# A graph layer pair on one core: 65 gather slots in place of 60, and the fullest tile's work moved behind the next indices

## What is computed

```python
h = jnp.maximum(_layernorm(x, axis=-1), 0.0)
# layer 1: attention over the neighbours, 4 heads of 32
Wh = (h @ W).reshape(N, H, D)
e = s_src[:, None, :] + s_dst[None, :, :]
e = jnp.where(e >= 0, e, ALPHA * e)
e = jnp.where(adj[:, :, None] > 0, e, NEG_INF)
attention = jax.nn.softmax(e, axis=1)
h_prime = jnp.einsum('ijh,jhd->ihd', attention, Wh)
x = x + jax.nn.elu(h_prime.reshape(N, H * D))
# layer 2: maximum over the neighbours
h = jnp.maximum(_layernorm(x, axis=-1), 0.0)
masked = jnp.where(mask[:, :, None], h[None, :, :], neg)
x = x + jnp.max(masked, axis=1)   # 0 where there is no neighbour
```

## Time and profile before

| | us |
|---|---|
| median of 3 runs | 491.2 (489.4 to 493.13) |
| the profiled execution, its own time | 493.0 |
| its span, first to last instruction | 491.0 |
| GpSimd busy | 328.1 (67%) |
| VectorE busy | 314.0 (64%) |
| TensorE products busy | 303.5 (62%) |
| ScalarE busy | 141.5 (29%) |

### The profile page before, as it was taken

How to read it: one execution, slowest core, us unless ns; L and a number is a source line. 1 busy time by engine, 2 the same in 40 slices (tenths; PEclk the granted TensorE clock), 3 DMA queues, 4 the chain that set the end, 5 groups by cost and what they waited for, 6 DMA issues and landing times. The chain is left out here.

```text
span 491.0 us, 6636 instructions
## 1 busy us (share of the span) xinstructions
PE 303.5 (62%) x2017; PEld 225.1 (46%) x2017; DVE 314.0 (64%) x1219; ACT 141.5 (29%) x330; POOL 328.1 (67%) x360
## 2 busy tenths in 40 slices
PE   0966567679789687689464521464565655466664
PEld 0833334266346353355354520354564544365653
DVE  6998876859869596779846382455444545454553
ACT  1653422131544538173733160010110101010111
POOL 6972673704777777767777225777777777777770
PEclk9989579689789699788775785588857788875688
DMA  7998699996999999993575011222222222222221
GB/s 263 420 368 348 237 319 380 404 366 237 369 342 371 404 400 404 403 401 124 183 245 165 12 66 53 53 55 53 58 56 63 66 65 64 73 62 75 69 72 45
DMA packets 28731, 100.86 MB, mean 205 GB/s; under 512 B 6869, under 2 KB 13397, under 8 KB 20501
## 3 DMA queue, kind: packets, MB, share of 16 engines
q1 hardware_dynamic: 16245, 76.33, 39.7%
q0 software_dynamic: 9344, 19.75, 15.6%
q10 hardware_dynamic: 3104, 4.33, 2.4%
HBM read 93.92 MB, written 6.46 MB: 204 GB/s over the span
## 5 line engine op out<-in xcount | busy, mean ns | idle before, releaser
L741 POOL DMA_INDIRECT G<-wh_table,idx x146 | 149.1, 1022 | 81.2 <-issue 43.3
L1641 POOL DMA_INDIRECT G<-h_table,idx x146 | 138.2, 946 | 49.1 <-issue 44.2
L1735 DVE TENSOR_TENSOR_SCAN S<-adjf,S,psf 128x512 f32<-128x512 bf16 (+2 forms) x38 | 45.9, 1209 | 85.8 <-PE psf L1666 76.0
L927 PE MATMUL psf<-adjf,packw 128*128 128x512 f16 x256 | 77.4, 446 | 17.5 <-DMA adjf<-in_adj_dram 12.9
L1666 PE MATMUL psf<-identf,G 128*128 128x128 f32 x146 | 31.8, 352 | 81.9 <-DMA G<-h_table,idx 81.9
L1651 ACT COPY Sb<-psf 128x512 f32<-128x512 f32 (+2 forms) x39 | 21.8, 558 | 168.4 <-PE psf L1674 168.4
L1666 PEld LDWEIGHTS psf<-identf,G 128*128 128x128 f32 x146 | 20.0, 173 | 90.4 <-DMA G<-h_table,idx 90.4
L1686 PE MATMUL psf<-Sb,OL 128*128 128x128 f32 x292 | 55.3, 351 | 0.3 <-DVE rows_out L1721 0.2
L1082 PE MATMUL psf<-G,OQ 128*128 128x132 f32 x292 | 48.6, 321 | 7.0 <-issue 5.0
L1686 PEld LDWEIGHTS psf<-Sb,OL 128*128 128x128 f32 x292 | 52.5, 268 | 0.7 <-issue 0.4
L927 PEld LDWEIGHTS psf<-adjf,packw 128*128 128x128 f16 x256 | 24.8, 107 | 55.6 <-issue 17.9
(11 more groups left out here) (188 smaller groups left out, 481.0 us busy)
## 6 DMA issues: line engine op xcount, KB each, us to landing
adjf<-in_adj_dram SPq DMA_DIRECT2D x64, 1024.0 KB, 11.5
adjf<-keep_table SPq DMA_DIRECT2D x4, 960.0 KB, 7.3
G<-wh_table,idx POOLq DMA_INDIRECT x146
G<-h_table,idx POOLq DMA_INDIRECT x146, 2.6
out_dram<-rows_out SPq DMA_DIRECT2D x32, 64.0 KB, 1.7
wh_table<-OQ ACTq DMA_DIRECT2D x7, 272.0 KB, 8.4
h_table<-h1b ACTq DMA_DIRECT2D x3, 384.0 KB, 2.3
xsf<-in_x_dram SPq DMA_DIRECT2D x2, 512.0 KB, 10.3
```

The costliest lines, as they stand in the source:

```text
L741: pool.indirect_dma_start(G[:, plan.at[k] + b, :], None, wh_table, bass.IndirectOffsetOnAxis(ap=idx[:, n:n + 1], axis=0)).then_inc(gathere ...
L927: nc.tensor.matmul(o, packw[:, k, :], bits, start=(k == 0), stop=False)
L1641: pool.indirect_dma_start(G1[:, g % NG, q, :], None, h1_table, bass.IndirectOffsetOnAxis(ap=idx[:, n0 + q:n0 + q + 1], axis=0)).then_inc(f ...
L1735: V.tensor_tensor_scan(S[:, g % 3, 0:w * P], flags[:, n0 * P:(n0 + w) * P], ps[:, g % 3, 0:w * P], start, ALU.mult, ALU.max).then_inc(scan ...
```

## The change

It changes no operation's arithmetic. It does four things.

- **Slots.** The ring has 65 blocks. Batch 4 gets slots of its own (50 to 64) and waits for no one (`free_after` -1). Batch 5 takes the hub's and waits for the hub's sum in place of batch 2's; batches 6 to 9 wait for the same batches as before. To make room `cand` moves into `near`, `prod` into `em`, and the rows that are stored move from `h1b` into the buffer of the exponentials, which alternates between `ex` and a part of `E2` (`ex_of`), with one store semaphore for each. `elus(k)` now waits until the store from the same buffer two batches before has landed.
- **Hub scores and maxima.** `scores(0)` and `scores(1)` move from the end of turns 1 and 2 to behind the masks of turns 2 and 3; `maxima` of both move behind `edges`, and the hub's `less_max` behind `take_words(3, 2)`. TensorE does `scores_by_row` of the hub behind `select` and `turn` and the hub's `max_back` right after, in turn 3.
- **Hub weighing and sums.** `weigh(1)` moves to turn 4, behind the indices of batch 4, with `weigh(2)` behind it; `aggregate(1)` follows in turn 4 of TensorE ahead of `aggregate(2)`.
- **Hub's end.** `finish(1)` stands at the end of turn 4, `finish_rest(1)` at the start of turn 5; GpSimd does the norms of the hub and of batch 2 both ahead of batch 5, and `h1_out(1)` comes in turn 5.

The core of the diff, without the renamed semaphores and the lines of ScalarE that follow the same order:

```diff
-        users = [[0, 1]] + [[k] for k in range(2, self.nb)]
...
-        self.ring = sum(room)
+
+        hubs, gap = self.size[0] + self.size[1], self.size[2] + self.size[3]
+        third = hubs + gap + self.size[4] - self.size[7]
+        self.at = [0, self.size[0], hubs, hubs + self.size[2], hubs + gap, 0, max(self.size[5:]), third, 0, max(self.size[5:])]
+        self.free_after = [-1, -1, -1, -1, -1, 1, 3, 4, 5, 6]
+        self.ring = hubs + gap + self.size[4]
...
-        cand = sbl("cand", [P, UK * BITS], I32)
+        assert SIZE * P >= 2 * UK * BITS
+        cand = near[:, :].bitcast(I32)[:, 0:UK * BITS]
...
-        prod = E2[:, 0:SK]
+        prod = em[:, :, :].rearrange("p k h -> p (k h)")[:, 0:SK]
...
-        h1b = sbl("h1b", [P, U, D])
...
+        def ex_of(k):
+
+            n = len(plan.tiles(k))
+            if k == 1:
+                return ex[:, U - n:U, :]
+            return E2[:, U * D:(U + n) * D].rearrange("p (t d) -> p t d", d=D) if k % 2 else ex[:, 0:n, :]
...
             for k in range(NBT + 3):
-                tl = plan.tiles(k - 3)
-                if tl:
-                    pool.wait_ge(var1_ready, 2 * (k - 3))
+                for j in (1, 2) if k == 5 else (k - 3,) if k > 5 else ():
+                    tl = plan.tiles(j)
+                    pool.wait_ge(var1_ready, 2 * j)
...
                     act.wait_ge(hp_ready, k)
-                    nc.scalar.activation(ex[:, 0:len(tl), :], hp[:, 0:len(tl), :], ACT.Exp).then_inc(ex_ready, 1)
+                    if k > 3:
+
+                        act.wait_ge(h1_stored[k % 2], 16 * ((k - 1) // 2))
+                    nc.scalar.activation(ex_of(k), hp[:, 0:len(tl), :], ACT.Exp).then_inc(ex_ready, 1)
...
                 pack_to(words_free(k - 1, 3))
-                if k <= NBT:
+                if 2 <= k - 2 <= NBT - 2:
                     max_back(k - 2)
                 if k < NBT:
                     select(k)
                     turn(k)
+                if 0 <= k - 2 < 2:
+                    scores_by_row(k - 2)
+                if k == 3:
+                    max_back(1)
...
-                    aggregate(k - 2)
+                    if k == 4:
+                        aggregate(1)
+                    if k - 2 > 1:
+                        aggregate(k - 2)
...
-                    if 0 <= k - 1 < NBT:
+                    if 2 <= k - 1 < NBT:
                         scores_by_row(k - 1)
...
-                together(*when(plan.tiles(k - 3), finish, k - 3))
+                if k == 5:
+                    together(finish_rest(1))
+                together(*when(k > 4 and plan.tiles(k - 3), finish, k - 3))
                 if k == 0:
                     split_scores()
-                together(*when(new, rows_of_edges, k), *when(0 <= k - 2 < NBT, distances_to_max, k - 2))
+                together(*when(new, rows_of_edges, k), *when(2 <= k - 2 < NBT, distances_to_max, k - 2))
+                together(*when(0 <= k - 2 < 2, scores, k - 2))
...
-                together(*when(plan.whole(k - 2), weigh, k - 2))
+                together(*when(k - 2 > 2, weigh, k - 2))
                 together(*when(new, edges, k))
+                if k == 4:
+                    together(weigh(1))
+                    together(weigh(2))
                 if 2 <= k < NBT:
                     line_ends(k)
+                together(*when(0 <= k - 2 < 2, maxima, k - 2))
...
                 take_words(k, 2)
+                together(*when(k - 2 == 1, less_max, k - 2))
                 take_words(k, 3)
                 together(*when(k + 1 < NBT, extract, k + 1))
-                together(*when(0 <= k - 1 < NBT, scores, k - 1))
+                if k == 4:
+                    together(finish(1))
+                together(*when(2 <= k - 1 < NBT, scores, k - 1))
```

More of the change, by code:

```diff
@@ L911, in _ @@
             h1_out(NBT - 1)
-            act.wait_ge(h1_stored, 16 * (NBT - 1))
+            for b in range(2):
+                act.wait_ge(h1_stored[b], 16 * len(range(2 - b, NBT, 2)))
         @block.tensor
```

45 lines of the change are left out of this document (24 added, 21 removed).

## The result

Measured side by side, the changed kernel takes 495.48 us (median of 11 runs, 491.78 to 497.17) and the kernel before 493.06 (11 runs, 489.05 to 496.65). The ratio is 1.0064, 95% interval 1.0035 to 1.0094: about 3.1 us slower. The profiled execution took 495.38 us, span 493.5, against a span of 491.0 before. The forecast was 1.1 us faster. A ratio leaves out runs that took over 1.5% longer than the fastest of their kernel, a median doesn't.

The account below looks back on a forecast made before the run. The prediction took second-pass gathers, begun after a first pass paced from about 160 us by the adjacency stream, as the bound. Stream -2.8, first pass's end +1.7, second pass 0 gave -1.1: 490.1 us against 491.2, range 486 to 495.

Parts of the forecast that it names:

- Indices, batches 3 and 4: First pass, GpSimd's gathers: batch 3 starts 11.0 us earlier at 104.6, batch 4 8.1 us earlier at 128.9.
- The hub's sums and pack 16: Turn 4 on TensorE: hub's sums begin at 129.6, take 5.67 us, and pack 16 is done at 141.0, not earlier.
- Turn 5: First pass on VectorE: turn 5 starts at 138.9, plus 1.5 us for the hub's exponentials.
- The stream: Adjacency loads pacing the first pass: earlier packs close holes before 126 us, gaining 2.8 us, between 0 and 5.7.
- End of the first pass: Last exponentials share a buffer and wait for batch 7's store: 1.7 us later, bounds 0 and 2.5.
- Second pass: The gathers of the second pass: untouched by the change, 0 us.
- Edits at nothing: Shared buffers (`cand` in `near`, `prod` in `em`), earlier store waits and batch 4's dropped wait cost nothing.
- The lead: Faster rival, chance 0.17: GpSimd's 8.1 us lead at batch 4 reaches the end, giving 484.8 us.
- Only the end changes: Rival, chance 0.20: pack 16 holds the stream to its present time, its term is 0, giving 492.9 us.
- The slower rival: Chance 0.11: hub's sums on TensorE at half clock take 12.3 us, pack 16 done at 147.7, giving 496.9 us.
- own range: Range of the forecast's sum alone, without the rivals: 487.5 to 493 us.
- The rule on the stream: By the skill's 435 GB/s ceiling, the stream has 3.3 us of headroom and follows an earlier packer: 486.8 us.

Follow-up runs that it names:

- e6: The changed kernel, unchanged, as a control on one chip with the kernel before; ratio 1.0088 to the kernel before.
- e4: The changed kernel with 22 extra products keeping TensorE busy in three idle stretches of turns 3 and 4; ratio 1.005 to the kernel before.
- the second pair: The kernel before (e5) and the changed kernel (e6), both unchanged, measured and traced on one chip; ratios 1.0015 and 1.0088.
- e7: The changed kernel with pack 16 ahead of the hub's sums, batch 5's offsets behind them, and own room for the last exponentials; ratio 1.0049 to the kernel before.
- e3: The changed kernel with the last batch's exponentials in room of their own, not waiting for batch 7's store; ratio 1.0023 to the kernel before.
- e1: Only the change's 65 slots and shared buffers, every stage in the order of the kernel before; ratio 1.0012 to the kernel before.
- e12: Slots and shared buffers in the order of the kernel before, plus own room for the last exponentials; ratio 1.0005 to the kernel before.
- e18: The same version as e12, run again; ratio 1.0008 to the kernel before.
- e11: As e7, and VectorE no longer waits at turn 5's start for the hub's exponentials; ratio 1.0012 to the kernel before.
- e5: The kernel before, unchanged, as a control with a trace of its own; ratio 1.0015 to itself.
- e8: As e7, with pack 17 also moved ahead of tile 1's sums on TensorE; ratio 1.013 to the kernel before.
- e2: The changed kernel with tile 14's words ahead of the hub's weighing and pack 16 ahead of the hub's sums; ratio 1.004 to the kernel before.

## Why the prediction was wrong, step by step

*Indices, batches 3 and 4.* Batch 3 was forecast at 104.6 and came at 105.9, batch 4 at 128.9 and came at 130.1, turn 4 at 118.1 and came at 119.2, the hole for the offsets was forecast as 5 us and was 5.28. Right, all 1.1 to 1.3 us late, though not by one lag. Batch 3 is late because turn 3 starts 1.0 us late. Turn 4 is late because pack 12 ran at half clock (3.27 + 0.60 us in place of 1.98 + 0.38). The hub's row sums went the other way: 5.26 us was their time at half clock, and they took 2.94. That they leave turn 4 only 1.1 us late is luck.

*The hub's sums and pack 16.* Forecast done at 141.0, measured 144.5. The hub was forecast to be weighed at 129.6 and was so at about 131.7 (127.89 plus 3.82): the lag of 1.1, and 1.0 us more because VectorE waited 2.52 us for a transpose behind pack 14, which ran at half clock (3.14 us). The sums began at 132.71, another 1.0 later, since pack 15 at half clock (3.60 + 0.60 in place of 1.98 + 0.38) held TensorE that long. The sums themselves took 6.22 in place of 5.67. I had looked for the clock's effect in the hub's sums alone. And pack 15 should have been read, not assumed: it ran at half clock in the kernel before too. Timeline of TensorE of the kernel before, then of e6, where it ran at full clock and the sums waited 1.34 us for the weighing:

```profile
130.32 3.60 PE L927 MATMUL psf<-adjf,packw 128*128 128x512 f16 x8 [2.12 <-ACT psf L749]
```

```profile
130.39 1.98 PE L945 MATMUL psf<-adjf,packw 128*128 128x512 f16 x8 [2.12 <-ACT psf L754]
```

The loss of e6 is no smaller (1.0088 against 1.0064), and e4 gained little, so this clock doesn't look like what lost the time.

*Turn 5.* This step fails: "Turn 5 starts at 138.9, plus 1.5 us for the hub's exponentials". The 138.9 answers to the scores of batch 3, measured at 140.37: late by little more than the lag. Between them and turn 5's first instruction the kernel before has 1.2 us (142.28 to 143.5) and the changed one 5.1 (140.4 to 145.5). The addition was 3.9, not 1.5: a wait of 2.77 and 1.0 of `finish_rest`, which I had struck from turn 4 and not put back. ScalarE's queue shows why the wait is long. The values were there at 140.0, but the exponentials stand behind the copy of tile 1's sums, the end lines and the sum of tile 15's words (that copy, then the exponentials):

```profile
141.85 0.27 ACT L854 COPY ag<-psf 128x132 f32<-128x132 f32 x1 [2.44 <-PE psf L1105]
...
143.29 0.29 ACT L846 ACTIVATE ex<-hp_f 128x128 f32<-128x128 f32 x1
```

So turn 5 starts 2.0 us later than in the kernel before (145.5 against 143.5, and 146.2 against 144.2 in the second pair), not 3 us earlier.

*The stream.* This term of the sum fails with it. The -2.8 rested on the two holes before 126 us, and those closed as forecast. It failed by what comes after: I took pack 16 for the only thing that could give the gain back, and read off turn 5 only its offsets. In the changed kernel pack 16 did open the hole (DMA share 0.43 in 138 to 147 us). But packs 18 and 19 stand behind turn 5's `select`, and e7 shows that with pack 16 out of the way they open another. The forecast of tile 27 near 200 was 204.34. In place of -2.8 the first pass was 0.8 us longer in one pair and 3.1 in the other. How much of that is turn 5's start stays open.

*End of the first pass.* Forecast +1.7. The wait before the last exponentials is 2.42 in place of 0.71 us, the stretch 1.45 longer, and own room takes the wait away (e3, e7). Right. The stretch of the second pair is 3.88 longer, for a reason that I had not foreseen (TensorE's clock, below).

*Second pass.* Forecast 0, measured -0.4 and 0.0.

*Edits at nothing.* Right within what the ratios tell: e1, e12, e18.

*The rivals.* The lead didn't carry through: 7.0 us at batch 4 (8.1 forecast), gone by batch 5. "Only the end changes" was nearer than the forecast and still lacked turn 5's start. The slower rival named the right place: pack 16 came behind 144, and there are holes in 142 to 150 us. But its price was the hub's sums at 12.3 us, and they took 6.2 (5.6 in e6, up to 8.2 in the slower groups); and the date that it hung on doesn't decide (e4, e11). No rival was the exponentials' wait, although the forecast carries its 1.5 us in a half sentence. I had given that half sentence no bound from above.

*The time itself.* The forecast of 490.1 stood on a median of 491.2 from three runs; eleven runs put it at 493.06. So of the 5.4 us between forecast and 495.48, 1.9 belong to the base and 3.5 to the change. The "own range" of 487.5 to 493 was also narrower than the bounds of its two terms, which give 485.5 to 493.7.

*The rule on the stream.* By it the stream would have had headroom and followed an earlier packer. It ran at 401 GB/s in 160 to 203 us as before, so no run used such headroom there, though other stretches ran faster (412 GB/s in 106 to 109 us and 425 in 116 to 119 of the changed kernel).

## What to carry to other kernels

A wait that is removed from one engine of a ring of stages was worth nothing here, since the ring was no shorter: add up that engine's idle time over all turns that the work was moved across, before and after (23.4 and 23.4 us here), and price each wait that the new order brings at the turn's boundary. Work that is postponed past a boundary carries its tail along: here the exponentials, the residual sum and one more norm. And where freed buffers are reused by a late stage, look at the last user, behind which nothing is left to hide a store.

## What the runs showed of the hardware that I had not expected

*TensorE's clock and short waits.* In the changed kernel pack 15 ran at half rate (3.60 us for 8 products, the lower level, 1.2 GHz) behind an idle time of only 1.76 us, and the granted clock was 0.52 in 120 to 126 us, ahead of it. But a low clock ahead isn't needed. In the kernel before, it was 1.00 in 120 to 126 us and 0.94 in 126 to 130; then TensorE idled 2.12 us, and pack 15 took 3.60 too. In e6 the same pack behind the same 2.12 us took 1.98. With 22 extra products in the idle stretches (e4) it took 1.98 behind 1.25 us. So a pause of some 2 us can cost the clock or not, in the same place of the program, and the rows don't show what decides. The Trainium skill ("TensorE: Matmul & The Clock Gate", "What's actually happening") says that the array falls to 1.2 GHz after idling, and that fits these rows; my reading of it, that a short pause does no harm, does not.

The clock also sets the end of the first pass. In its first trace TensorE idled 4.16 us ahead of the last scores and the next six products took 1.53 us; in e5 it had no such idle time and six took 0.84. Timelines of TensorE, first the first trace, then e5:

```profile
273.99 0.84 PE L1037 MATMUL psf<-identf,ee 128*48 128x128 f32 x3 [4.16 <-DVE ee L1388]
274.62 1.53 PE L1082 MATMUL psf<-G,OQ 128*128 128x132 f32 x6
```

```profile
273.52 0.84 PE L1082 MATMUL psf<-G,OQ 128*128 128x132 f32 x6
```

From the transposes of the last scores (L1037, at 272.93 in e5) to the last batch's sums the first trace takes 7.29 us and e5 4.88, and that is the whole difference in the stretch from last gather to second pass, 26.99 and 24.58 us. Of the twenty traces eleven have these six products near 1.53 us and nine near 0.84; the changed kernel has 1.53 in all three of its traces, the kernel before in one of two. Whether the change shifts that pause or chance does, three traces can't tell. It moves the time by 2.4 us, as much as the change under study. One pair of traces has a difference of spans of 2.5 us and the other of 7.7; 2.4 of the 5.2 between them lie here, 2.3 in the first pass.

*One kernel, two speeds 10% apart.* The kernel before takes 491 to 493 us in some groups of runs and 538 to 542 in others. What sets the speed stays open: e1 to e4 (540.5) and e5 to e8 (491.4) are even recorded with the same chip number. In the slower groups GpSimd's gathers wait for something that the trace doesn't name (second pass of e2: releaser, us in total, count, longest), and the second pass takes 220 to 224 us in place of 193:

```profile
POOL G L1679 <- remote: 19.3, 8, 3.3
```
